# Layer 3 mixer: scaling, projecting and turning of the first tiles in another order

## The reference, cut to what matters

```
h = _layernorm(x, axis=-1) * (1 + ca) + sa
q = (x @ Wq).reshape(b, s, 2 * H, D)      # x is h here; H = 8, D = 8
k = (x @ Wk).reshape(b, s, 2 * H, D)
v = (x @ Wv).reshape(b, s, H, 2 * D)
q = _rotary(q)
k = _rotary(k)
attn1 = _sdpa_over_heads(q1, k1, v)
attn2 = _sdpa_over_heads(q2, k2, v)
a = attn1 - lam * attn2
a = a * rms * ln_w + ln_b
x = x + ga * (a.reshape(b, s, E) @ Wo)
```

## Time and profile before

| | |
|---|---|
| median of 3 runs | 1147.49 us (1145.3 to 1154.59) |
| the profiled execution | 1150.39 us, span of its instructions 1149.1 us |
| busy over the span | PE 921.6, DVE 837.8, ACT 633.5, POOL 518.8 us |
| granted TensorE clock, mean | 0.891 |
| from the first turned tile of this mixer to its first weighed sum | 917.5 to 975.3 us |
| in that stretch (57.8 us) busy | PE 41.49, DVE 43.48, ACT 38.84, POOL 38.77 us |

### The profile page before, as it was taken

One profiled execution on the slowest core, in us unless ns is written; L12 is line 12 of the kernel. 1 busy time (PEld: TensorE's weight loads), 2 busy tenths in 40 slices (PEclk: granted clock), 3 DMA queues, 4 the chain that ended last, 5 costly groups with the idle time before them and its releaser, 6 DMA issues. The chain is left out here.

```text
span 1149.1 us, 18561 instructions
## 1 busy us (share of the span) xinstructions
PE 921.6 (80%) x5611; PEld 561.4 (49%) x5611; DVE 837.8 (73%) x1639; ACT 633.5 (55%) x1368; POOL 518.8 (45%) x505
## 2 busy tenths in 40 slices
PE   5997799999677866568888888877999276978991
PEld 3532344544445543222223232256999254866981
DVE  6788999999999467778777787167544459886333
ACT  3478799897243353317666667835544266235432
POOL 2047799899501413301111121125563458426773
PEclk9888899999877997759999999968999679968996
DMA  9000000000000300510011110043110200001114
GB/s 321 1 1 1 1 1 1 1 1 1 1 1 0 147 1 17 148 29 12 22 29 30 29 29 2 3 186 104 41 45 25 83 1 1 1 32 42 52 48 124
DMA packets 28014, 46.29 MB, mean 40 GB/s; under 512 B 8720, under 2 KB 16408, under 8 KB 26896
## 3 DMA queue, kind: packets, MB, share of 16 engines
q1 hardware_dynamic: 22672, 34.66, 9.7%
q0 software_dynamic: 4096, 8.35, 2.5%
q10 hardware_dynamic: 1152, 2.10, 0.5%
HBM read 34.45 MB, written 12.58 MB: 41 GB/s over the span
## 5 line engine op out<-in xcount | busy, mean ns | idle before, releaser
L2116 DVE TENSOR_REDUCE sb_l_mxp<-ps 128x2 f32<-128x1024 f32 (+3 forms) x152 | 171.3, 1163 | 42.1 <-PE ps L1929 37.9
L1057 POOL TENSOR_TENSOR sb_gs<-sb_hs,sb_xp 128x512 f32<-128x512 f32 x128 | 162.3, 1302 | 18.0 <-PE ps L685 12.9
L2059 ACT ACTIVATE sb_l_pT<-ps 128x512 f32<-128x512 f32 (+3 forms) x256 | 111.4, 519 | 77.2 <-PE ps L1984 76.0
L685 PE MATMUL ps<-sb_gs,sb_ident 128*128 128x512 f32 x256 | 132.2, 607 | 0.2
L3080 PE MATMUL ps<-sb_hT,sb_f_shared 128*128 x936 | 118.6, 276 | 1.9 <-ACT sb_hT L3113 1.9
L3080 PEld LDWEIGHTS ps<-sb_hT,sb_f_shared 128*128 128x128 f32 x936 | 110.8, 192 | 3.1 <-issue 2.5
L1984 PE MATMUL ps<-sb_l_qk 51*128 51x512 bf16 (+3 forms) x384 | 88.9, 335 | 18.3 <-ACT sb_l_pT L2059 8.3
L3121 ACT ACTIVATE sb_f_hid<-ps 128x512 f32<-128x512 f32 x78 | 46.6, 597 | 74.0 <-PE ps L3080 73.9
L3180 POOL DMA_INDIRECT moe_y<-sb_f_rows,sb_f_rowi x64 | 64.0, 1000 | 51.7 <-DVE sb_f_rows L3152 37.3
L3091 PE MATMUL ps<-sb_sw_f_out,sb_f_hid 128*128 x624 | 82.7, 276 | 0.9 <-DVE sb_f_hid L3141 0.6
L959 ACT ACTIVATE sb_dA<-sb_dt,sb_negA 128x512 f32<-128x512 f32 x109 | 77.8, 713 | 7.2 <-DVE sb_hs L862 6.6
(11 more groups left out here) (415 smaller groups left out, 2097.8 us busy)
## 6 DMA issues: line engine op xcount, KB each, us to landing
sb_sw_f_in<-w_f_in SPq DMA_DIRECT2D x2, 2048.0 KB, 9.9
sb_sw_f_out<-w_f_out SPq DMA_DIRECT2D x2, 2048.0 KB, 12.4
sb_l_qk<-spill SPq DMA_DIRECT2D x112, 32.0 KB
spill<-sb_l_parts SPq DMA_DIRECT2D x12, 256.0 KB, 3.0
moe_y<-c_f_zero SPq DMA_DIRECT2D x1, 2048.0 KB, 9.9
sb_sw_f_up<-w_f_up SPq DMA_DIRECT2D x1, 2048.0 KB, 12.2
moe_h<-sb_f_rows SPq DMA_DIRECT2D x8, 256.0 KB, 4.4
sb_f_rows<-moe_y SPq DMA_DIRECT2D x8, 256.0 KB, 6.0
```

Source lines behind the costliest of these rows:

```text
L685: pe.matmul(ps[:, 4 + e * CPB + hf, :], ident[:], gs[:, p % SL, :], start=False, stop=n == DS - 1).then_inc(acc, 1)
L1057: gp.tensor_tensor(gs[:, q % SL, :], hs[:, q % SL, :], cs[:, k % 2, hf * CH:(hf + 1) * CH], ALU.mult).then_inc(times_c, 1)
L2059: ac.activation(pT[e % 3][:, h, 0:width], ps[:, bank[n_bank], 0:width], ACT.Exp, scale=L2_SCALE).then_inc(exped, 1)
L2116: dv.tensor_reduce(dst, src, AX_X, ALU.max).then_inc(max_out, 1)
```

## The change

Three things change in the mixer of layer 3, and no arithmetic.

- PE projects tiles 0 and 1 right behind turned(0), which suffices since both lie in chunk 0. The other chunks are turned one at a time: turned(1) behind project(1), turned(2) behind rotate(0) and project(2), turned(3) behind rotate(1) and project(3). Chunk c is turned into bank 0, 2, 3, 2 for c = 0 to 3, as banks 0 and 1 now hold projections; turned(3) therefore waits for the features of chunk 1. values(0), values(1) and values(2) come together behind project(4).
- ACT takes modulate_chunk(t) ahead of scale(t) for t = 0 to 3, and the exponential of `lam` ahead of scale(4).
- The buffers `v` and `sc` are laid out ahead of `qk` and `turned2`.

```diff
--- before.py
+++ after.py
@@ -191,11 +191,11 @@
                 i = pe.transpose(ps[:, c, t * P:(t + 1) * P], xn[:, c * TPC + t, :], ident[:])
             i.then_inc(ln_tr, 1)
 
-    def modulate_chunk(layer, part, nth, c):
+    def modulate_chunk(layer, part, nth, c, bank=None):
 
         b = c * CH // S
         ac.wait_ge(ln_tr, NCH * nth + c + 1)
-        ac.activation(hT[:, c * CH:(c + 1) * CH], ps[:, c, :], ACT.Identity,
+        ac.activation(hT[:, c * CH:(c + 1) * CH], ps[:, c if bank is None else bank, :], ACT.Identity,
                       scale=modF[:, layer, part * 2 + 1, b:b + 1],
                       bias=modF[:, layer, part * 2, b:b + 1]).then_inc(ln_hT, 1)
 
@@ -2278,15 +2278,15 @@
 
         ROT = 4
         PAIRS = D3 // 2
+        v = sb("l3_v", [P, NT, H3, E3], ctx=ctx)
+        sc = sb("l3_sc", [P, NT, 2, H3, H3], ctx=ctx)
         qk = sb("l3_qk", [P, ROT, 2 * NQ, D3], ctx=ctx)
         turned2 = sb("l3_rc", [P, 2, 2, 2 * NQ, D3], ctx=ctx)
         raw = lambda t, k: ps[:, t % 2, k * 2 * D:(k + 1) * 2 * D].rearrange("p (h d) -> p h d", d=D3)
         rotated = lambda t: ps[:, ROT + t % ROT, 0:2 * D].rearrange("p (h d) -> p h d", d=D3)
         v_bank = lambda t: (2, 3, 0, 1)[t // TPC]
         v_ps = lambda t: ps[:, v_bank(t), t % TPC * D:(t % TPC + 1) * D].rearrange("p (h e) -> p h e", e=E3)
-        v = sb("l3_v", [P, NT, H3, E3], ctx=ctx)
         pr = sb("l3_pr", [P, 4, 1024], ctx=ctx)
-        sc = sb("l3_sc", [P, NT, 2, H3, H3], ctx=ctx)
         st = sb("l3_st", [P, NT, 2, H3], ctx=ctx)
         own = lambda c: c % CPB == CPB - 1
         summed_ps = lambda c: (TPC - own(c)) * P
@@ -2313,6 +2313,7 @@
         V0, WO = NT // 2 + NCH, B
 
 
+        turned_bank = lambda c: (0, 2, 3, 2)[c]
         score_pool = lambda t, c: c == 1 or t % 2 == 1
         weigh_pool = lambda t: t % TPB in (1, 3, 4, 6)
         SUMS = [b * TPB + t for b in range(B) for t in (1, 3, 0, 2, 4, 6, 5)]
@@ -2403,18 +2404,19 @@
         def tensor():
             def turned(c):
                 normalised(pe, 6, c)
+                if c == 3:
+                    features(pe, 6, 1)
                 for t in range(TPC):
-                    i = pe.transpose(ps[:, c, t * P:(t + 1) * P], xn[:, c * TPC + t, :], ident[:])
+                    i = pe.transpose(ps[:, turned_bank(c), t * P:(t + 1) * P], xn[:, c * TPC + t, :], ident[:])
                 i.then_inc(ln_tr, 1)
 
             pe.wait_ge(*ld["rest"])
             turned(0)
-            turned(1)
 
             def project(t):
                 if t >= 2:
                     pe.wait_ge(rot_out, ROT0 + t - 1)
-                features(pe, 6, max(t // TPC, t if t < 2 else 0))
+                features(pe, 6, t // TPC)
                 pe.matmul(ps[:, t % 2, :], hT[:, t * P:(t + 1) * P], wqkv[:, 0:W1],
                           start=True, stop=True).then_inc(qkv_mm, 1)
 
@@ -2434,15 +2436,17 @@
             pe.wait_ge(signed, SIGNED)
             project(0)
             project(1)
-            turned(2)
-            turned(3)
+            turned(1)
             for t in range(NT):
                 rotate(t)
                 if t + 2 < NT:
                     project(t + 2)
-                if t < TPB:
+                if t < 2:
+                    turned(t + 2)
+                elif t < TPB:
                     features(pe, 6, NCH - 1)
-                    values(t)
+                    for late in range(0 if t == 2 else t, t + 1):
+                        values(late)
             pe.wait_ge(rot_out, ROT0 + NT)
             for t in range(TPB, NT):
                 i = values(t)
@@ -2491,10 +2495,12 @@
             ac.wait_ge(*ld["rest"])
             flip = wqkv[:, 2 * D:W1].rearrange("p (i s) -> p i s", s=2)[:, :, 0]
             ac.activation(flip, flip, ACT.Copy, scale=-1.0).then_inc(*a_step.up())
-            modulate(3, 0, 6)
-            ac.wait_ge(lam_v, 1)
-            ac.activation(lam[:, 0:2], lam[:, 0:2], ACT.Exp).then_inc(*a_step.up())
             for t in range(NT):
+                if t < NCH:
+                    modulate_chunk(3, 0, 6, t, turned_bank(t))
+                if t == NCH:
+                    ac.wait_ge(lam_v, 1)
+                    ac.activation(lam[:, 0:2], lam[:, 0:2], ACT.Exp).then_inc(*a_step.up())
                 scale(t)
                 if t > 0:
                     copy_rotated(t - 1)
```

## The result

The changed kernel takes 1143.69 us as the median of 20 runs (1139.69 to 1150.37), the kernel before 1149.98 in 20 runs taken beside it (1143.36 to 1156.21). The ratio is 0.9953, 95% interval 0.9934 to 0.9972: 5.4 us less, between 3.2 and 7.6. The medians differ by 6.3 us. That is clear of the scatter and within 1%.

A forecast was written before the change was run, and what follows sets the result against it. It took ACT's late first scale to bound the mixer head. 1150.4 - 6.2 (earlier scale(4)) + 0.9 (slower sums) gave 1145.1 for the profiled execution; with -5.5 typical, the middle of 1144.9 and 1142.0, 1143.5 us, range 1137 to 1149.

The forecast's parts named there:

- What bounds the kernel: Mixer head: ACT's late scale(0) holds up the chain; ACT bounds at 1.95 us a tile until DVE's product of tile 6.
- Projections: Tiles 0 and 1 need only chunk 0; two projections cost 3.41 us, scale(0) starts 8.5 us earlier.
- The clock: Mixer head: PE's unbroken work raises the clock at about 923.8; it should stay fast, rotate and project taking 0.86 each.
- The ping-pong: Tiles 0 to 3: ACT needs 2.8 us per tile, PE 2.2 at the fast clock, so ACT leads.
- term of -6.2: Gain at scale(4) in the mixer head, starting at 934.0 instead of 940.25.
- The sums: PE's 224 weighed sums: 4.8 us of slow clock instead of 2.9, costing +0.9 us.
- The sum: Whole kernel: 1150.4 - 6.2 + 0.9 = 1145.1 for the profiled execution; -5.5 us taken, 1143.5 forecast, chance 0.70.
- the prediction's last sentence: Outside the mixer head: a span differing by more than 3 us would mean scatter, not the change, sets the time.
- Rival 1: Mixer head: clock stays slow until the last chunk is turned; scale(4) gains 2.9 instead of 6.2; chance 0.15.
- the rule set beside it: PE's turned chunks: transposes don't count as clock activity, so the rise comes late and the gain is 2.9, not 6.2.
- Rival 2: Behind tile 6: DVE or POOL takes the gain back, none of the 6.2 arrives, 1147 to 1150 us; chance 0.10.
- Rival 3: Mixer tiles: slow clock makes PE cost 3.85 us a tile against ACT's 1.95; a loss; chance 0.05.

The follow-up runs named there:

- e5: Changed kernel with one extra exponential in ScalarE's wait for the first turned chunk, so the table loads there; ratio to the kernel before 0.9949.
- e8: Kernel before with three extra TensorE products behind turned(3), filling its wait for scale(0); ratio to the kernel before 0.9993.
- e3: Changed kernel with turned(2) and turned(3) put back directly behind turned(1), ahead of rotate(0); ratio to the kernel before 0.9968.
- e1: Kernel before with only the new layout, v and sc ahead of qk and turned2; ratio to the kernel before 1.0006.
- e2: Changed kernel with ScalarE's old order, tiles 0 and 1 still projected early, other chunks turned in a row; ratio to the kernel before 1.0006.
- e9: Changed kernel with seven extra TensorE products filling its wait ahead of the weighed sums; ratio to the kernel before 0.9909.
- e11: Changed kernel with 20 extra transposes ahead of turned(0), where e6 had three products; one run, end of sums 76.6 us behind the first features.
- e6: Changed kernel with three extra TensorE products ahead of turned(0), in TensorE's idle time; ratio to the kernel before 0.9947.
- e7: Changed kernel with the additions of both e5 and e6; ratio to the kernel before 0.9936.
- e10: e7 with POOL's first head product held until DVE has normed chunk 3 and its wog products taken behind that; ratio to the kernel before 0.9895.
- e12: Changed kernel with the additions of e10 and e9 together; ratio to the kernel before 0.9928.

## Why the prediction was right, point by point

**What bounds the kernel.** Right. The head of the mixer was one chain from ScalarE's first scale on, and what ScalarE gained at scale(4), W kept: 6.8 and 6.9 us in the change, 2.0 and 1.8 in e5, 2.9 and 2.9 in e8.

**Projections.** A small miss. scale(0) was put at +2.6 and came at +3.0. The first project starts 0.92 and not 0.8 behind the features, and the two take 3.75 us to the end of the last where the chain's 3.41 had been used.

**The clock.** It was put at a rise 4.4 us behind the first project, and rose 5.3 behind it, at F + 6.2, inside the bound of 6.6. The reason given for its staying fast was an average over 21 us, with PE busy for three quarters. e3 shows that such an average secures nothing: TensorE's longest wait since the clock's rise was 1.53 us there, and the clock fell. The step held for this order and was not secured by its argument.

**The ping-pong.** ScalarE led, as predicted, and TensorE and the norms lay beside it. Its period was put at 2.8 us and measured 2.5 to 2.6 (919.81, 922.38, 924.89), since a feature step takes 0.68 and a scale 1.57 from start to start when the next instruction overlaps it. That is why scale(4) came at +14.8 and not +15.4, although scale(0) was 0.4 late. The term of -6.2 was -6.8.

**The sums.** The slow clock there was 4.25 us where 4.8 was assumed, and the term of +0.9 was +0.6. In the runs that did not fill the wait ahead of the sums it lay between 2.9 and 5.6 us. The prediction called this luck; with one profile of each kernel the runs can't tell luck of the execution from the kernel's own timing (before, e1 and e2, with the same W, all have 2.9 to 3.0). e9 shows what it costs.

**The sum.** -5.3 for the profiled execution was -6.3 in the mixer; the -5.5 taken for the medians stands against 5.4 from the ratio (3.2 to 7.6). 1143.5 against 1143.69 is partly luck: the prediction started from about 1149.0, 1.0 below the median of 20 runs, and took 5.5 off where the medians differ by 6.3, and the two misses nearly cancel. It is also closer than the method allows: the profile's own two executions differ by 4.4 us ahead of F, which by the prediction's last sentence would let scatter set the time. It does so for single executions, and it took 20 runs of each to see the change.

**The rivals.** Rival 1, a clock kept slow by the turned chunks, fell with the windows of the changed kernel, and the rule set beside it with e11. Rival 2, a gain taken back by DVE or POOL behind tile 6, fell with the unchanged 27 us from that product to W, and with e5. What the prediction did not see is a collision of DVE's norm of chunk 3 with POOL's first head product, which costs nothing in the change (the norm of chunk 3 takes 1.52 us as before) but held up e6 and e7, until e10 took it away. Rival 3 had no sign: ScalarE waits for no project after the first.

**Named too narrowly.** The prediction explained the gain by scale(0) standing earlier. e8 splits it: 2.9 of 6.9 us are TensorE's clock, which stays up in the new order; that order leaves no wait like the 4.3 us of the earlier trace rows behind the turned chunks. In the prediction that part lay inside the -6.2 and was not priced apart.

## What to carry to other kernels

Where an engine runs its queue in order, look for the first tile's instruction and what stands ahead of it that it does not need; here a moved scale was worth 6.8 us, an early projection nothing, and a misplaced exponential of 0.2 us would have cost 5.2, the clock behind it included. A wait of TensorE shortly ahead of work on the critical chain costs twice, by itself and by the clock behind it: fill it or break it up, and price the clock as a term of its own. A filling must end before the work behind it is due: in e12 the early one held turned(0) back by 0.7 us. Put table loads into an engine's idle time, and once an engine is made to start earlier, look at which shared resource its followers will then hold.

## What the runs showed of the hardware

- The granted clock rose 2.9 to 6.0 us after TensorE took up work in these traces, and the same 224 matmuls took 25.8 us at the fast clock and 26.7 to 27.9 us with a slow start. In e3 it fell though no wait of TensorE since its rise was longer than 1.53 us; from 928.40 to 931.85 TensorE was busy for 1.70 us.
- Transposes alone raised the clock, after 4.2 us (e11, one execution).
- A table load of 1.28 us took 1.6 us of ScalarE's time (e5).
- Four DVE tensor_scalar of 128 x 128 took 1.08 us beside POOL's 128 x 4 steps alone, 1.52 beside POOL's two products of 128 x 128 and 2.60 when a product of 128 x 512 followed these; held apart, 1.12 again.
